# Four results per token summed up at the end of a mixture-of-experts layer: rows read in 4 KB pieces into places of their own, and half of the sums made on TensorE

## The reference, cut to what matters

```python
def _L1_ffn_ref(hidden, router_w, expert_bias, gate_w, up_w, down_w, shared_gate_w, ...):
    flat = hidden.reshape(-1, 256)                       # 2048 tokens
    scores = jnp.sqrt(jax.nn.softplus(flat @ router_w.T))
    _, idx = jax.lax.top_k(scores + expert_bias, 4)
    topv = jnp.take_along_axis(scores, idx, axis=1)
    topv = topv / (topv.sum(axis=-1, keepdims=True) + 1e-20)
    probs = zeros.at[arange(T)[:, None], idx].set(topv)
    for each expert e:
        acc = acc + probs[:, e:e+1] * _clamped_swiglu(flat, wg[e], wu[e], wd[e])
    return acc + _clamped_swiglu(flat, shared_gate_w, ...)
```

## Time and profile before

| | |
|---|---|
| median of 3 runs | 700.75 us (700.16 to 700.87) |
| the profiled execution | 701.65 us, with a span of 699.9 us |
| TensorE, matmuls | 581.5 us busy, 83% of the span |
| VectorE | 448.3 us, 64% |
| ScalarE | 385.2 us, 55% |
| GpSimd | 377.6 us, 54% |
| DMA | 155.02 MB, mean 221 GB/s |
| last load of a tile's rows issued | 656.22 us |
| last result of a tile copied by ScalarE | 671.87 us |
| last instruction of VectorE begins | 695.2 us |

### The profile page before, as it was taken

The page is one execution under the profiler, slowest core; times in us unless marked ns, Lnnn a source line. Parts: engine busy times, 40 slices in busy tenths (PEclk is TensorE's granted clock), DMA queues, the critical chain, the costliest instruction groups (busy, mean ns, idle before and its releaser), DMA issues.

```text
span 699.9 us, 14308 instructions
## 1 busy us (share of the span) xinstructions
PE 581.5 (83%) x4069; PEld 468.0 (67%) x4069; DVE 448.3 (64%) x1392; ACT 385.2 (55%) x1132; POOL 377.6 (54%) x527
## 2 busy tenths in 40 slices
PE   1588899999989999979997896864878999999920
PEld 0487787787767777868775674643667787788710
DVE  1546647676767866668566665653755777555596
ACT  1002456765777667865567956742445666566610
POOL 6847847366464475686545336161355565555560
PEclk9999999999999999998999899985889999999965
DMA  7989999999999993222345955764344555555779
GB/s 269 247 223 334 335 334 334 330 325 332 316 310 329 318 309 112 77 79 76 106 134 176 403 166 162 276 222 129 116 121 134 156 163 150 153 160 160 218 259 306
DMA packets 135740, 155.02 MB, mean 221 GB/s; under 512 B 15248, under 2 KB 124944, under 8 KB 135408
## 3 DMA queue, kind: packets, MB, share of 16 engines
q1 hardware_dynamic: 117536, 122.50, 58.4%
q0 software_dynamic: 7632, 20.98, 8.3%
q10 hardware_dynamic: 10496, 10.62, 4.8%
HBM read 53.92 MB, written 100.28 MB: 220 GB/s over the span
## 4 chain that ended last, share of the span: by engine, by line
PE 65%; DVE 10%; POOL 8%; ACT 6%; issue 6%; DMA 4%; another core or an unknown queue 1%; SPq 0%; ACTq 0%; DVEq 0%; POOLq 0%
PE ps L387 12%; PE pc L650 10%; PE pS L354 6%; POOL arena L1373 4%; PE pS L630 4%; PE ps L432 3%; PE ps L616 3%; DMA work<-y_rows 2%; PE po L601 2%; PE ps L562 2%; PE ps L493 2%; PE ps L472 2%; PE po L377 2%; PE ps L476 2%; DMA stage<-xn_rows 2%
## 5 line engine op out<-in xcount | busy, mean ns | idle before, releaser
L650 PE MATMUL pc<-arena,tk 128*128 128x128 f32 x768 | 108.3, 294 | 13.3 <-POOL arena L1373 7.3
L650 PEld LDWEIGHTS pc<-arena,tk 128*128 128x128 f32 x768 | 96.6, 201 | 25.7 <-issue 13.5
L387 PE MATMUL ps<-arena,work 128*128 x380 | 102.1, 393 | 1.4 <-ACT work L1132 1.4
L1373 POOL TENSOR_TENSOR arena<-arena 128x512 f32<-128x512 f32 x64 | 90.5, 1428 | 21.0 <-ACT arena L1178 20.8
L1387 POOL DMA_INDIRECT expert_rows<-stage,ixl x64 | 63.8, 996 | 53.2 <-DVE ixl L1007 20.4
L1245 ACT ACTIVATE work<-pS,work 128x128 f32<-128x128 f32 x256 | 72.7, 369 | 2.9 <-DVE work L909 2.6
L706 DVE TENSOR_SCALAR work<-ps 128x256 f32<-128x256 f32 x95 | 40.0, 421 | 50.5 <-PE ps L387 48.4
L387 PEld LDWEIGHTS ps<-arena,work 128*128 128x128 f32 x380 | 67.2, 197 | 7.4 <-issue 1.8
L354 PE MATMUL pS<-arena,tk 128*128 x190 | 61.6, 407 | 8.5 <-ACT tk L1127 6.9
L1122 ACT ACTIVATE tk<-work 128x128 f32<-128x128 f32 x95 | 29.4, 310 | 63.1 <-DVE work L706 53.3
L909 DVE TENSOR_REDUCE work<-pS 128x4 f32<-128x512 f32 x64 | 43.8, 685 | 25.4 <-PE pS L630 25.4
(11 more groups left out here) (286 smaller groups left out, 1442.7 us busy)
## 6 DMA issues: line engine op xcount, KB each, us to landing
expert_rows<-stage SPq DMA_DIRECT2D x32, 2080.0 KB, 21.3
work<-expert_rows SPq DMA_DIRECT2D x95, 130.0 KB
arena<-in_w SPq DMA_DIRECT2D x8, 1536.0 KB
stage<-xn_rows SPq DMA_DIRECT2D x64, 130.0 KB
xn_rows<-xnD ACTq DMA_DIRECT2D x16, 512.0 KB
work<-y_rows SPq DMA_DIRECT2D x16, 512.0 KB
tk<-in_tk SPq DMA_DIRECT2D x1, 2048.0 KB, 9.6
out<-xs SPq DMA_DIRECT2D x16, 128.0 KB, 3.4
```

What stands on the lines that cost most here:

```text
L387: i = pe.matmul(p[U * k:U * k + U, 0:256], xgT[n % 3][:, 128 * c + U * k:128 * c + U * k + U], arena[:, 256 * c:][:, bass.ds(e, 256)], sta ...
L650: i = pe.matmul(pv, tk[:, h, 128 * d:128 * d + 128], kvv[:, ci, :, :].rearrange("p b (i h j) -> p (b i) h j", i=8, h=8)[:, :, hl, :], star ...
L1373: pool.tensor_tensor(kv[kk % 4][:, c, half, :].rearrange("p (i h j) -> p i h j", h=8, i=8), i0, i1, ALU.mult).then_inc(s_kv, 1)
```

## The change

It changes where a result row lands, how and when the rows are read back, and who sums them.

- **New order.** Choice k of token p of batch b now has row `512 + 2048 k + 16 p + b`. A partition's 16 batches lie one behind the other, so a load of four batches has one piece of 4 KB per partition. Only the host's table changes for that.
- **A place for each choice.** k = 3 goes to the four buffers `rb` as before. k = 2 goes to `stage` (7 batches) and to the first 2304 columns of `arena` (9 batches), the weights of experts 0 to 2, as soon as TensorE has finished tile 73 (`GONE3`). k = 1 and k = 0 go to `arena` further up (`far`), k = 1 when TensorE has finished all 95 tiles, k = 0 right behind it. None of the loads waits for VectorE.
- **Half of the batches on TensorE.** Batches 0 to 7 stay on VectorE: 32 instructions. For batches 8 to 15 ScalarE makes 32 scaled identities, 128x128 each (identity times the column `pk4[:, b, k]`), after its last tile. TensorE multiplies each with the batch's 256 columns and sums the four choices in one PSUM bank per batch, 32 matmuls after its last tile. VectorE adds each bank to `xs`: 8 instructions behind its 32.
- **Output.** 8 stores of two batches each in place of 16 of one.

```diff
+        diag = [arena[:, 2304 + 128 * n:2432 + 128 * n] for n in range(KT * HALF)]
+        far = [arena[:, 6400 + 4096 * k:10496 + 4096 * k].rearrange("p (b d) -> p b d", d=256) for k in range(2)]
...
+        GONE3 = EARLY + 3 * NB
+        PIECES = [(0, NS, stage[:, :, 0:256]), (NS, NB, arena[:, 0:256 * (NB - NS)].rearrange("p (b d) -> p b d", d=256))]
+
+        def result(k, b):
+            if k == 2:
+                n = [n for n, (b0, b1, p) in enumerate(PIECES) if b0 <= b < b1][0]
+                return PIECES[n][2][:, b - PIECES[n][0], :], (d_in[n], 64)
+            g = b // 4
+            if k == 1:
+                return far[k][:, b, :], (d_g[g], 16 * (-(-(NT - g) // 4) + 1))
+            if k == 0:
+                return far[k][:, b, :], ((d_pk, d_tk, d_qp, d_skip)[g], (48, 32, 32, 32)[g])
+            return rb[g][:, b % 4, :], (d_st[g], 16 * (SC[g] + 1))
...
+            pe.wait_ge(s_c, NT)
+            pe.wait_ge(s_gT, NT)
+            pe.wait_ge(s_hT, NT)
+            accs = [*gbanks, *xbanks, po, *ybanks, banks.tiles[2]]
+            for k in range(KT - 1, -1, -1):
+                for n in range(HALF):
+                    if k == KT - 1 and n == HALF - 3:
+                        pe.wait_ge(s_y, NT)
+                    if k == KT - 1 and n == HALF - 1:
+                        pe.wait_ge(s_acc, NB)
+                    rows_, there = result(k, HALF + n)
+                    pe.wait_ge(*there)
+                    pe.wait_ge(s_dg, HALF * (KT - 1 - k) + n + 1)
+                    i = pe.matmul(accs[n][:, 0:256], diag[HALF * k + n], rows_, start=(k == KT - 1), stop=(k == 0))
+                    if k == 0:
+                        i.then_inc(s_cmb, 1)
...
             dve.wait_ge(s_routed, 1)
-            for m in range(4 * KT):
-                g, k = m % 4, KT - 1 - m // 4
-                dve.wait_ge(d_st[g], 16 * (SC[g] + m // 4 + 1))
-                for i in range(4):
-                    b = 4 * g + i
-                    if m < 4:
-                        dve.wait_ge(s_acc, b + 1)
-                    else:
-                        dve.wait_ge(s_fin, 4 * (m - 4) + i + 1)
-                    dve.scalar_tensor_tensor(out=xs[:, b, :], in0=rb[g][:, i, :], scalar=pk4[:, b, k:k + 1], in1=xs[:, b, :],
-                                             op0=ALU.mult, op1=ALU.add).then_inc(s_fin, 1)
+            for k in range(KT - 1, -1, -1):
+                for b in range(HALF):
+                    rows_, there = result(k, b)
+                    dve.wait_ge(*there)
+                    dve.wait_ge(s_acc, b + 1 if k == KT - 1 else NB + HALF * (KT - 2 - k) + b + 1)
+                    dve.scalar_tensor_tensor(out=xs[:, b, :], in0=rows_, scalar=pk4[:, b, k:k + 1], in1=xs[:, b, :],
+                                             op0=ALU.mult, op1=ALU.add).then_inc(s_acc, 1)
+            accs = [*gbanks, *xbanks, po, *ybanks, banks.tiles[2]]
+            for n in range(HALF):
+                dve.wait_ge(s_cmb, n + 1)
+                dve.tensor_tensor(xs[:, HALF + n, :], accs[n][:, 0:256], xs[:, HALF + n, :], ALU.add).then_inc(s_acc, 1)
...
+            act.wait_ge(s_routed, 1)
+            for k in range(KT - 1, -1, -1):
+                for n in range(HALF):
+                    act.activation(diag[HALF * k + n], ident, ACT.Copy, scale=pk4[:, HALF + n, k:k + 1]).then_inc(s_dg, 1)
...
-            for m in range(4 * KT):
-                g, k = m % 4, KT - 1 - m // 4
-                if m == 0:
+            for k in range(KT - 1, -1, -1):
+                if k == KT - 1:
                     sp.wait_ge(s_acc, NB)
-                if g == 0:
-                    sp.wait_ge(s_st, last[k])
-                    sp.sem_inc(s_thr, 1)
-                if m >= 4:
-                    sp.wait_ge(s_fin, 4 * (m - 4) + 4)
-                o = DUMP + NB * 128 * k + 512 * g
-                sp.dma_start(rb[g], Yr[o:o + 512, :].rearrange("(b p) d -> p b d", p=128)).then_inc(d_st[g], 16)
+                sp.wait_ge(s_st, last[k])
+                sp.sem_inc(s_thr, 1)
+                yk = Yr[DUMP + NB * 128 * k:DUMP + NB * 128 * (k + 1), :].rearrange("(p b) d -> p b d", b=NB)
+                if k == 2:
+                    sp.wait_ge(s_yp, GONE3)
+                    for n, (b0, b1, place_) in enumerate(PIECES):
+                        sp.dma_start(place_, yk[:, b0:b1, :]).then_inc(d_in[n], 16)
+                    continue
+                if k == 1:
+                    sp.wait_ge(s_yp, NT)
+                for g in range(4):
+                    sp.dma_start(rb[g] if k == 3 else far[k][:, 4 * g:4 * g + 4, :],
+                                 yk[:, 4 * g:4 * g + 4, :]).then_inc(((d_pk, d_tk, d_qp, d_skip), d_g, None, d_st)[k][g], 16)
             ov = out.rearrange("b d l -> d b l")
-            for b in range(NB):
-                sp.wait_ge(s_fin, NB * (KT - 1) + b + 1)
-                sp.dma_start(ov[:, b, :], xs[:, b, :]).then_inc(d_out, 16)
-            sp.wait_ge(d_out, 16 * NB)
+            for b in range(0, NB, 2):
+                sp.wait_ge(s_acc, NB + HALF * (KT - 1) + b + 2)
+                sp.dma_start(ov[:, b:b + 2, :], xs[:, b:b + 2, :]).then_inc(d_out, 16)
+            sp.wait_ge(d_out, 16 * HALF)
...
-    dest[:, 0] = 512 + np.arange(KT * NB * 128)
+    dest[:, 0] = 512 + np.arange(KT * NB * 128).reshape(KT, 128, NB).transpose(0, 2, 1).reshape(-1)
```

More of the change, by code:

```diff
@@ L15 @@
 NB = 16
+HALF = NB // 2
 NE = 32
@@ L296, in build @@
         (s_rw, s_rwP, s_regs) = (sem(n) for n in ("s_rw", "s_rwP", "s_regs"))
-        (s_gP, s_gT, s_gup, s_c, s_t, s_m, s_h2, s_hP, s_hT, s_yp, s_y, s_fin) = (sem(n) for n in (
-            "s_gP", "s_gT", "s_gup", "s_c", "s_t", "s_m", "s_h2", "s_hP", "s_hT", "s_yp", "s_y", "s_fin"))
+        (s_gP, s_gT, s_gup, s_c, s_t, s_m, s_h2, s_hP, s_hT, s_yp, s_y, s_cmb, s_dg) = (sem(n) for n in (
+            "s_gP", "s_gT", "s_gup", "s_c", "s_t", "s_m", "s_h2", "s_hP", "s_hT", "s_yp", "s_y", "s_cmb", "s_dg"))
         banks = Banks([ctx.enter_context(nc.psum_tensor(f"ps{i}", [128, 512], F32)) for i in range(4)], (d_id, 16))
```

## The result

The changed kernel takes 695.49 us, the median of 5 runs (693.30 to 697.29), against 700.75 us (698.94 to 701.64, 5 runs) of the kernel before: a ratio of 0.9931, with a 95% interval of 0.9904 to 0.9958. It is faster, by 0.7%; the forecast was 695.9 us. The profiled execution, the slowest of the five, took 697.29 us with a span of 695.2, 4.7 us less than the 699.9 of before.

The account below looks back on a forecast made before the run. Places and bytes together were taken to bound the end, with DMA the limit from 671 to 688 us. TensorE's 673.8 + 5 + 11.4 = 690.2, addition to 690.8, plus 4.2 gave span 695.0, median 695.9; range 691.8 to 700.2.

Parts of the forecast that it names:

- Loads of k = 3 and 2: Start of the read-back: k = 3 issued at 657.11 us, k = 2 following at about 659, 4.2 MB queued instead of 2.1.
- Rate: Speed of the read-back loads in 4 KB pieces: 390 GB/s taken, between bounds of 349 and 404.
- What they hold up: Last tiles' stores, slowed by the load burst: tile 94's copy 1.1 us late at 673.0, TensorE's last tile about 0.8 late.
- Rival B: At the loop's end, the burst starves stores: tile 90's copy waits, end slips 4.4 us, median 699.2 us; chance 0.20.
- Loads of k = 1: Read-back after the loop: leaves when TensorE finishes tile 94, 672.5 us; issue at 671.5 to 673 would confirm it.
- The clock: TensorE's 32 final matmuls: 5 us at half clock (5.9 matmuls), then 11.4 us for the other 26.1 at full clock.
- Rival C: TensorE's final sums: the clock does not return, all 32 matmuls at half clock, median 706.7 us, slower; chance 0.07.
- D: Read-back loads: the new order is slow to read, rate halved to 200 GB/s, median near 708.4 us; chance 0.03.
- Identities: ScalarE after its last tile: at most 0.29 us each, about 9 us for 32, or 12 at 0.38; under TensorE's 16.4.
- Behind the last sum: Kernel's end: 4.2 us after the last addition for last stores and their landing, kept from before; perhaps 3.2.
- What costs nothing: In the end stage, VectorE's 32 instructions finish under TensorE's end, and 8 stores instead of 16 save unneeded SP queue time.
- the hole and the pieces: Ground of the gain: filling the low-rate stretch at 666 to 671 us (90 and 119 GB/s), and faster 4 KB load pieces.

Follow-up runs that it names:

- e0: The changed kernel with the four load thresholds as constants instead of read from a table: 683.38 us against 688.14, ratio 0.9927 to the kernel before.
- e1: e0 with the old order of result rows and so 1 KB load pieces again: ratio 0.9913 to the kernel before.
- e3: e0 with the loads of k = 2 held until the last tile is done: ratio 0.9907 to the kernel before.
- f1: e0 without the ten stores of result rows of tiles 85 to 94: ratio 0.9895 to the kernel before.
- f3: e0 with all sixteen batches summed on VectorE and without the ten stores of tiles 85 to 94: ratio 0.9954 to the kernel before.
- h2: e0 with seven result-row buffers instead of five and four GpSimd stores under way instead of three: 678.67 us against 687.20, ratio 0.9887.
- h3: h2 with the identities of k = 3 and 2 made during the loop and five batches of both summed before the last-tile wait: ratio 0.9920 to the kernel before.
- f2: e0 with seven buffers of result rows instead of five: ratio 0.9958 to the kernel before.
- e2_all_vector: e0 with all sixteen batches summed on VectorE, without identities or TensorE sums: 695.87 us, ratio 1.0090 to the kernel before.
- i1_skip: e0 with rows that hold no token left out of the stores by an index beyond the tensor: ratio 0.9978 to the kernel before.

## Why the prediction was right, and where not

The time was right, 695.9 against 695.49 us, and so was the span, 695.0 against 695.2. That it fits so closely is in part luck: the copy of tile 94 came 1.25 us later than forecast and the clock 1.5 us sooner, the end behind the last sum had the right size for another reason, and the profiled execution was 0.9 us above its median before and 1.8 after. The steps are as follows.

- *Loads of k = 3 and 2.* Forecast at about 659 us for k = 2, found at 659.74; four plus two loads in the queue at once. Right.
- *Rate.* 390 GB/s taken; 356 to 666 us and 408 behind, 389 beside TensorE's sums. Right on the whole.
- *What they hold up.* The copy of tile 94 was to come at 673.0, it came at 674.25 after waits of 0.68, 2.10 and 1.40 us for stores. The mechanism was right, the term half of what it is: 2.4 us later than in the kernel before, where 1.1 were forecast. What isn't so is that TensorE's last tile is late with it. Rival B, with tile 90 late by 4.4 us, didn't happen: tile 90 was copied at 666.00 (665.85 before), and its ground, larger packets that take the stores' share, made no difference between e0 and e1.
- *Loads of k = 1.* 672.5 forecast, 671.34 found, just outside the 671.5 to 673 that were to show it: TensorE's last tile ended at 671.30 us and was not held by the late copies.
- *The clock.* 5 us at half clock taken; TensorE began at 675.06, and its fifth matmul, at 678.53, ran at the full clock: 3.5 us. The 1.5 us less at half clock give back about 0.75 of what the late start took, and the last matmul ended at 690.8 against 690.2. Rival C is refuted, as is D: the new order was read at 408 GB/s.
- *Identities.* At most 0.29 to 0.38 us each; 9.44 us for 32, 0.295 each. Not in the way.
- *Behind the last sum.* 4.2 us were kept from the kernel before, as last stores and their landing; 4.0 were found (691.24 to 695.2). The size is right and the reason wrong. The five runs whose last step waits 0.2 us and that have eight stores (e3, f1, f3, h2, h3) need 2.6 to 2.9 us for the output. The rest here is the wait for GpSimd.
- *What costs nothing.* The forecast held GpSimd to be without work in this part but for the last tiles. These last tiles are the point: their stores, with these inputs of rows that nobody reads, hold the copies during the loads and then the end.

What the forecast gave as the ground of the gain, the hole and the pieces, is not what gained. Undone one at a time, neither loses anything that can be measured (e1, e3); with the pieces 12% slower to arrive and the end in the same place, the DMA engines, which the forecast took for the limit of the end, are not the limit in the changed kernel. What does gain is the half of the sums on TensorE: without it the other parts together are 0.9% slower than the kernel before. In the profiles that loss is GpSimd's; with its late stores gone TensorE's half is still worth 4.7 us (f1, f3). This is shown for each part alone, in the presence of the others. That the places without a wait for VectorE carry the rest was not tried by itself, nor was TensorE's half on the kernel before. The wait for GpSimd behind a long row of VectorE's sums, a mechanism by which this change without TensorE's half is a loss, was among none of the rivals.

That GpSimd's last store sets the end is shown by f1, f2 and h2: taken away, the late wait goes; the sums made earlier, it grows; the stores made earlier, it goes again. What GpSimd does in the 11 to 15 us between its last store's start and its end, of which the store's landing is some 6 to 7 us, the profile doesn't name.

## What to carry to other kernels

Before a sum is made for the end of a kernel, list every engine that has to finish, with its last instruction and how long its end takes; an engine that is far from busy can be the last, and a part that gains in one place is then paid back there. Where a burst of loads is moved earlier, look for the small transfers of another queue that have to land in the meantime, and give them buffers and semaphores to spare before the burst grows. And where VectorE is to run two-input operations without a gap, keep GpSimd's stores out of that stretch or give a part of the work to TensorE.

## What the runs showed of the hardware that I had not expected

- **A row of VectorE's two-input operations can hold up GpSimd's making of a store.** 21.89 us for one store in e2_all_vector, ending 0.8 us behind VectorE's row; 5.25 us in the kernel before, also ending 0.8 us behind its row; 2.03 to 4.61 us in eight runs with shorter rows; 0.95 to 1.3 us otherwise. Others that met such a row were not held, as the 1.27 us at 669.48 in the kernel before. The Trainium skill, "SBUF — State Buffer", section "Who interferes with whom", says that a VectorE instruction with two SBUF inputs contends with a GpSimd instruction that reads SBUF; the store reads its row numbers there, and the trace agrees for the stores that were held, not for the others. The same section infers that such an operation doesn't stop the making of descriptors; for `scalar_tensor_tensor` back to back this trace shows a store that as a whole does wait, and doesn't show which part of it.
- **A small store beside a burst lands some 6 to 7 us after GpSimd has made it, with or without data.** For the 131 KB of tile 90 it was 6.0 us in e0_changed and 668.17 - (658.87 + 2.13) = 7.2 us in f2_seven (by the program's wait), and in i1_skip, where its rows move no bytes, 6.4 us.
- **Pitch and pieces.** Partitions 16 KB apart, read in 4 KB pieces, came at 401 to 414 GB/s; rows 128 KB apart in 1 KB pieces at 353 to 365.
